# FFN of a decoder layer: one matmul per token with the high and low weight products side by side, copied out by ScalarE, summed and weighted on GpSimd

## What is computed

```python
sx, ix = top_k(sim[0], 8); sy, iy = top_k(sim[1], 8)          # 8 heads, 32 keys on each side
scores, pk = top_k(sx[..., :, None] + sy[..., None, :], 8)    # 8 of 64 pairs per head
indices = take(ix * 32 + iy, pk)                              # experts, 0 to 1023
h = gelu(einsum('bnd,bnhkd->bnhk', x, down_embed[indices]))
h = softmax(scores) * h
out = einsum('bnhk,bnhkd->bnd', h, up_embed[indices])
x = layernorm(x + out)
```

## Time and profile before

| | us |
|---|---|
| median of 3 runs (lowest, highest) | 1327.79 (1326.99, 1329.32) |
| the profiled execution: its own time | 1325.4 |
| its span | 1323.7 |
| busy in the span: PE, DVE, ACT, POOL | 1155.8, 1159.2, 865.3, 636.4 |
| the part `ffn` (from its first instruction on the chain) | 1026.96 to 1323.7 |

### The profile page before, as it was taken

The page is one execution under the profiler, slowest core; times in us unless marked ns, Lnnn a source line. Parts: engine busy times, 40 slices in busy tenths (PEclk is TensorE's granted clock), DMA queues, the critical chain, the costliest instruction groups (busy, mean ns, idle before and its releaser), DMA issues. The chain is left out here.

```text
span 1323.7 us, 32659 instructions
## 1 busy us (share of the span) xinstructions
PE 1155.8 (87%) x12752; PEld 901.2 (68%) x12752; DVE 1159.2 (88%) x2866; ACT 865.3 (65%) x1195; POOL 636.4 (48%) x534
## 2 busy tenths in 40 slices
PE   3576999999999999999999999999997739877778
PEld 2463677777777777777777777777776728767678
DVE  5797899989999899999989999998986688999984
ACT  0346888888888888988888888887974342212121
POOL 2344667566775757767566775757430310000000
PEclk9768999999999999999999999999999776666666
DMA  7006999999999999999999999999998300000000
GB/s 158 1 6 135 196 194 185 200 198 196 200 194 193 190 199 200 197 195 186 199 200 202 192 197 196 190 181 182 185 189 140 104 1 2 5 6 6 5 5 6
DMA packets 671123, 185.79 MB, mean 140 GB/s; under 512 B 655828, under 2 KB 668536, under 8 KB 670840
## 3 DMA queue, kind: packets, MB, share of 16 engines
q1 hardware_dynamic: 670968, 183.71, 81.5%
HBM read 19.51 MB, written 0.82 MB: 15 GB/s over the span
## 5 line engine op out<-in xcount | busy, mean ns | idle before, releaser
L1051 PE MATMUL ps<-pT,xa_hi 128*128 128x128 f16 x2288 | 381.1, 217 | 20.9 <-DMA pT<-p 20.6
L856 ACT ACTIVATE e<-ps,bias 128x1444 f32<-128x1444 f32 (+1 forms) x208 | 305.7, 1470 | 133.5 <-DVE bias L928 132.6
L1047 PE MATMUL ps<-pT,xa_hi 128*128 128x128 f16 x2288 | 382.8, 217 | 6.0 <-ACT uT L879 5.6
L1048 PE MATMUL ps<-pT,xa_lo 128*128 128x128 f16 x2288 | 382.8, 217 | 0.0
L926 DVE TENSOR_REDUCE nmax<-ps 128x1 f32<-128x1444 f32 (+1 forms) x208 | 343.9, 1653 | 21.0 <-PE ps L1031 20.3
L938 DVE TENSOR_TENSOR p<-e,p 128x1408 f16<-128x1408 f32 (+3 forms) x288 | 304.3, 1097 | 33.5 <-ACT p L864 32.2
L864 ACT ACTIVATE p<-e 128x1408 f16<-128x1408 f32 (+1 forms) x208 | 288.2, 1385 | 13.3
L811 POOL TENSOR_TENSOR p<-e,p 128x1408 f16<-128x1408 f32 (+1 forms) x128 | 196.6, 1557 | 182.6 <-ACT p L864 182.6
L1047 PEld LDWEIGHTS ps<-pT,xa_hi 128*128 128x128 f16 x2288 | 222.2, 98 | 30.2 <-issue 15.9
L1051 PEld LDWEIGHTS ps<-pT,xa_hi 128*128 128x128 f16 x2288 | 222.1, 98 | 27.1 <-DMA pT<-p 26.3
L1029 PE MATMUL ps<-xT_hi,q_hi 128*128 128x512 f16 (+1 forms) x624 | 229.2, 367 | 8.9 <-DMA xT_lo<-xa_lo 7.1
(11 more groups left out here) (235 smaller groups left out, 1928.2 us busy)
## 6 DMA issues: line engine op xcount, KB each, us to landing
raw<-in_ctx SPq DMA_DIRECT2D x16, 704.0 KB
pT<-p SPq DMA_TRANSPOSE x416, 4.2
f_wq<-in_L_ffn_w_q SPq DMA_DIRECT2D x1, 1024.0 KB, 5.0
f_wqt<-in_ffn_wq_t SPq DMA_DIRECT2D x2, 512.0 KB, 6.6
raw<-in_ctx SPq DMA_DIRECT2D x48, 18.0 KB
x_tok<-in_x SPq DMA_DIRECT2D x1, 800.0 KB
out_x<-ost SPq DMA_DIRECT2D x6, 128.0 KB, 2.1
wk_t<-in_wk_t SPq DMA_DIRECT2D x1, 512.0 KB, 5.4
```

Source lines behind the costliest of these rows:

```text
L856: act.activation(e32[t % E_BUF][rows, :], score_banks(t)[rows, 0:T], ACT.Exp, bias=bias[rows, t % N_BUF:t % N_BUF + 1]).then_inc(e_done, 1)
L1047: pe.matmul(out, hi, ph, start=n == 0, stop=False)
L1048: pe.matmul(out, lo, ph, start=False, stop=False)
L1051: pe.matmul(out, hi, pl, start=False, stop=False)
```

## The change

Per token column there is one matmul in place of two: the moving side is 32 columns, the high and low products side by side in one tile `mv`, and the two results are no longer summed in PSUM. A group is now 16 columns s (512 columns of PSUM), so a step has eight groups. ACT copies each group from PSUM to one of two SBUF tiles `g_sb` (`rows_out`). POOL adds the two halves (`g_sum`) and multiplies with gelu (`weigh`, two instructions per group). DVE has no part in it. The orders become:
- PE: `hidden(i,0)`, groups 0 to 3, `hidden(i,1)`, groups 4 to 7, then as before. Group g waits until group g-2 has been copied out (`g_out`), and no longer until it has been weighed.
- ACT: gelu 0, copies 0 to 3, gelu 1, `picks`, copies 4 to 7, `last_norm(i-2)`, exp, then as before. Copy g waits for POOL's sum of group g-2 (`sum_ready`).
- POOL: `combine(i)`, `norm_rstd(i-2)`, then eight times sum and product of step i-1. After the loop: the four groups of step 6, then `norm_rstd(5)`, `norm_rstd(6)`.

Two pairs of semaphores are merged into one each (`total_done` with `mean_done`, `simc_hi` with `simc_done`), with wait values to match. The core of the diff:

```diff
-        QP = 32
+        QP = 16
-        mv_hi, mv_lo = sb("mv_hi", [P, 2 * NC, PAD], F16), sb("mv_lo", [P, 2 * NC, PAD], F16)
+        mv = sb("mv_both", [P, 4 * NC, PAD], F16)
+        g_sb, g_sum = [sb(f"g_sb{i}", [P, 512]) for i in range(2)], sb("g_sum", [P, 2 * NC, QP])
...
+            def weigh(i, n):
+                nh, w = step_shape(i)
+                g, nb = group_number(i, n), nh * NC
+                both = g_sb[g % 2][:, 0:2 * nb * QP].rearrange("e (s x c) -> e x c s", x=2, c=nb)
+                pool.wait_ge(g_out, g + 1)
+                if g:
+                    pool.wait_ge(g_done, g)
+                pool.tensor_tensor(out=g_sum[:, 0:nb, :], in0=both[:, 0, :, :], in1=both[:, 1, :, :], op=ALU.add).then_inc(sum_ready, 1)
+                if n == 0:
+                    pool.wait_ge(gel_done, 2 * i + 2)
+                if i and n == 0:
+                    pool.wait_ge(y_ps, i)
+                pool.wait_ge(sum_ready, g + 1)
+                at = slice(n * QP, (n + 1) * QP)
+                pool.tensor_tensor(out=wgt[:, :, 0:nh * w].rearrange("e c (a s) -> e a c s", a=nh)[:, :, :, at],
+                                   in0=g_sum[:, 0:nb, :].rearrange("e (a c) s -> e a c s", c=NC),
+                                   in1=gel[i % 2][:, :, 0:nh * w].rearrange("e c (a s) -> e a c s", a=nh)[:, :, :, at],
+                                   op=ALU.mult).then_inc(g_done, 1)
...
+            def rows_out(i, n):
+                nh, w = step_shape(i)
+                g, used = group_number(i, n), 2 * nh * NC * QP
+                act.wait_ge(g_ps, g + 1)
+                if g >= 2:
+                    act.wait_ge(sum_ready, g - 1)
+                act.activation(g_sb[g % 2][:, 0:used], ps[:, 5 + g % 2, 0:used], ACT.Copy).then_inc(g_out, 1)
...
                 hidden(i, 0)
+                if i:
+                    for n in range(groups(i - 1) // 2):
+                        rows_out(i - 1, n)
+                hidden(i, 1)
+                picks(i)
+                if i:
+                    for n in range(groups(i - 1) // 2, groups(i - 1)):
+                        rows_out(i - 1, n)
                 if i >= 2:
                     last_norm(i - 2)
-                hidden(i, 1)
-                picks(i)
...
                 if g >= 2:
-                    pe.wait_ge(g_done, g - 1)
+                    pe.wait_ge(g_out, g - 1)
                 for q in range(QP):
                     s = n * QP + q
-                    dst = ps[:, 5 + g % 2, q * nb:(q + 1) * nb]
-                    pe.matmul(dst, oneh[0:j, :, s], mv_hi[0:j, 0:nb, s], start=True, stop=False)
-                    last = pe.matmul(dst, oneh[0:j, :, s], mv_lo[0:j, 0:nb, s], start=False, stop=True)
+                    last = pe.matmul(ps[:, 5 + g % 2, q * 2 * nb:(q + 1) * 2 * nb], oneh[0:j, :, s], mv[0:j, 0:2 * nb, s], start=True, stop=True)
```

More of the change, by code:

```diff
@@ L1067 @@
 PAD = P + 4
+STEP_GROUPS = P // 16
 def step_shape(i):
@@ L1140, in ffn @@
             sem(n) for n in ("f_waited", "fc_done", "ones_done", "x2T_ps", "x2T_done", "xcT_done"))
-        total_done, mean_ps, mean_done, xc_done, cov_ps, cov_done = (
-            sem(n) for n in ("total_done", "mean_ps", "mean_done", "xc_done", "cov_ps", "cov_done"))
+        mean_chain, mean_ps, xc_done, cov_ps, cov_done = (
+            sem(n) for n in ("mean_chain", "mean_ps", "xc_done", "cov_ps", "cov_done"))
         cw_ps, cw_done, sum_done, var_done, vrs_done, gain_done, kscaled_done = (
             sem(n) for n in ("cw_ps", "cw_done", "sum_done", "var_done", "vrs_done", "gain_done", "kscaled_done"))
-        simc_ps, simc_hi, simc_rest, simc_done = (sem(n) for n in ("simc_ps", "simc_hi", "simc_rest", "simc_done"))
+        simc_ps, simc_rest, simc_done = (sem(n) for n in ("simc_ps", "simc_rest", "simc_done"))
         simw_ps, simw_done, wide_act, wide_pool, narrow_done = (
@@ L1154, in ffn @@
         wide_idx, soft_done = sem("wide_idx"), sem("soft_done")
+        g_out, sum_ready = sem("fg_out"), sem("fsum_ready")
         block = ctx.enter_context(nc.Block())
@@ L1176, in group_number @@
         def group_number(i, n):
-            return 4 * i + n
+            return STEP_GROUPS * i + n
         def spread(v, nh):
@@ L1246, in _ @@
                     norm_rstd(i - 2)
+                if i:
+                    for n in range(groups(i - 1)):
+                        weigh(i - 1, n)
+            for n in range(groups(NSTEP - 1)):
+                weigh(NSTEP - 1, n)
             norm_rstd(NSTEP - 2)
@@ L1266, in _ @@
             act.wait_ge(simc_ps, 1)
-            act.activation(sim_c[0:1, :], ps[0:1, 6, :], ACT.Copy).then_inc(simc_hi, 1)
+            act.activation(sim_c[0:1, :], ps[0:1, 6, :], ACT.Copy).then_inc(simc_done, 1)
             def first_out(p):
@@ L1337, in _ @@
                 act.activation(w_hi[0:j, 0:w], ps[0:j, 4, 2 * P:2 * P + w], ACT.Copy).then_inc(selT_done, 1)
+            for n in range(groups(NSTEP - 1)):
+                rows_out(NSTEP - 1, n)
             last_norm(NSTEP - 2)
@@ L1342, in _ @@
         def _(dve):
-            dve.tensor_tensor(out=total[:, :], in0=x2sum[:, :], in1=x2[:, B - 1, :], op=ALU.add).then_inc(total_done, 1)
+            dve.tensor_tensor(out=total[:, :], in0=x2sum[:, :], in1=x2[:, B - 1, :], op=ALU.add).then_inc(mean_chain, 1)
             dve.wait_ge(mean_ps, 1)
@@ L1402, in _ @@
             scaled_keys(1)
[L1404 to L1416, removed]
             def norm_stats(i, part):
@@ L1502, in step @@
                 ins.then_inc(best_done, 1)
-                if i:
-                    weigh(i - 1, 2)
                 dve.wait_ge(best_done, 2 * i + 2)
@@ L1562, in step @@
                 dve.wait_ge(wlo_done, 2 * i + 1)
-                for wx, dst in ((w_hi, mv_hi), (w_lo, mv_lo)):
+                for wx, at in ((w_hi, 0), (w_lo, nb)):
                     if wx is w_lo:
                         dve.wait_ge(wlo_done, 2 * i + 2)
-                    ins = dve.tensor_tensor(out=dst[0:j, 0:nb, 0:w], in0=eqc[0:j, 0:nb, 0:w],
+                    ins = dve.tensor_tensor(out=mv[0:j, at:at + nb, 0:w], in0=eqc[0:j, 0:nb, 0:w],
                                             in1=wx[0:j, 0:w].rearrange("p (a s) -> p a s", a=1).to_broadcast([j, nb, w]), op=ALU.mult)
@@ L1574, in _ @@
             norm_shift(NSTEP - 2)
-            for n in range(groups(NSTEP - 1)):
-                weigh(NSTEP - 1, n)
             for part in range(3):
@@ L1613, in _ @@
             pe.wait_ge(cov_done, 1)
-            pe.wait_ge(mean_done, 1)
+            pe.wait_ge(mean_chain, 2)
             pe.wait_ge(wq_ld, 16)
@@ L1624, in _ @@
             sim_weights(0)
-            pe.wait_ge(simc_done, 1)
+            pe.wait_ge(simc_done, 2)
             pe.wait_ge(xcT_done, 1)
@@ L1695, in _ @@
                 if i:
-                    expert_rows(i - 1, 0)
-                    expert_rows(i - 1, 1)
+                    for n in range(groups(i - 1) // 2):
+                        expert_rows(i - 1, n)
                 hidden(i, 1)
                 if i:
-                    expert_rows(i - 1, 2)
-                    expert_rows(i - 1, 3)
+                    for n in range(groups(i - 1) // 2, groups(i - 1)):
+                        expert_rows(i - 1, n)
                 if i + 1 < NSTEP:
```

14 lines of the change are left out of this document (5 added, 9 removed).

## The result

The changed kernel takes 1351.36 us (median of 4 runs, 1350.01 to 1352.51), the kernel before 1328.55 beside it. The ratio is 1.017, with a 95% interval of 1.0149 to 1.019: slower by some 23 us, and 9 us above the upper end of my range.

A forecast was written before the change was run, and what follows sets the result against it. DVE and PE were nearly full, PE late by about 1.2 us a step. Step 1 -2.6, steps 2 to 5 +0.8 and the end +1.2 gave -0.6 on 1327.8: 1327.2 us, range 1321 to 1342 (8 in 10).

The forecast's parts named there:

- the price of POOL's instruction: POOL's sum and product per group of 256 float32 elements: 0.72 us each, a stride costing nothing to doubling.
- t: The moment from which a step is measured: the end of `mv_lo`, where PE can start the rows.
- the lock: POOL and DVE shutting each other out: the selection chain's first instruction with two SBUF inputs waits 0.4 us.
- My sign of being wrong: The forecast is wrong if DVE does not wait for `esc`, or POOL's products run beyond t + 20.
- POOL is dearer: Rival, chance 0.22: dearer sums before copy 7 delay exp and hit the selection chain; 1342 us at 0.9.
- a rival of its own (0.10): Selection chain on DVE: `idxf`, shifts and casts wait for POOL too, 0.4 us more a step; 1329 to 1331.
- PE's 8 us: Row matmuls: half of 256 a step go, freeing 8 us, but PE is late by only about 1.2.
- the end: Step 5's rows against short step 6: `oneh` 21.9 after t, last rows 7.9 us; loss 1.2 with rounding.
- Step 1: First step, without norm: exp ends at t + 15.8, `oneh` starts at about 23.4 instead of 26.0; gain 2.6.
- DVE reaches `ssum` at t + 17.5 now and could at t + 15.3: DVE loses four weighings, 2.4 us a step, three before `ssum`, but there it waits 2.7 to 3.1 for exp.

The follow-up runs named there:

- exp_first: The changed kernel, strides kept, with exp moved ahead of copies 4 to 7 in ACT's queue; 1345.96 us, 1.0122 of the kernel before.
- hi_product: Changed kernel with turned copies, four `g_sb`, groups 0 and 1 earlier on POOL, no low products, no POOL sum; 1312.16 us, 0.9878 of the kernel before.
- sum_runs: The changed kernel with POOL's sum going through the copy in its own order, leaving one strided product input; 1338.61 us, 1.0068 of the kernel before.
- early_four_flat: The changed kernel, plain copies, with four `g_sb` buffers and POOL doing group 0 before `comb`, group 1 before `frs`; 1334.03 us, 1.004 of the kernel before.
- copy_turns: The changed kernel with ACT's copy turning each group, so that POOL has no stride; 1333.49 us, 1.003 of the kernel before.

## Why the prediction was wrong

**The step that failed is the price of POOL's instruction**: "I take 0.72, as `x2sum` is the only one with two full float32 inputs and output", with the stride put at "nothing to doubling" in the bounds and at nothing in the sum. It measured 1.10 for the sum. Without strides the same sum measured 0.75, 0.73 in an undisturbed row, so the rest of the term was right: all of this term's miss is the stride. The Trainium skill (GPSIMD Engine Reference, section 3.1), which I had weighed against the rows, gives by my estimate 0.76 for this size; the unstrided 0.73 to 0.75 is close, and that estimate has nothing for a stride.

**How it grew.** Up to sum 5, at the end of which copy 7 can start, POOL ran for 11.4 us instead of 8.6 (t + 7.1 to t + 18.5). Of these 2.8 us more, six sums at some 0.38 too much make 2.3. The rest is in gaps: I took 1.5 us for a group of two instructions of 0.72; the rows show 2.1 for 1.16 and 0.73, gaps of 0.2. POOL waits for its own last result between them, and the wait for `g_done` ahead of each sum I did not price at all. Exp therefore came 3.1 us later than forecast (t + 21.5), as it stands behind copy 7 in ACT's queue, and the chain from `ssum` to the end of `sel` took 6.3 instead of 5.4, 0.5 more than the 0.4 that I had put down for the lock. Forecast t + 25.5 for `oneh`, found t + 29.1 (1206.24), against 25.3 before: four such steps are 15 us. My sign of being wrong was there: POOL's last product ran on to t + 24.1, far beyond t + 20.

**The rival was right, its weight was not.** "POOL is dearer" named the place (the sums before copy 7), the mechanism (exp behind the copies, then the lock) and the price: 1342 at an average of 0.9, some 30 us at 1.1. The average is (1.10 + 0.83) / 2 = 0.96, which would be 19 us on the line between these two; 23 were measured, and I put the rest down to the gaps. I gave it 0.22 because "the pair sums have patterns as complex and show no surcharge"; but those repeat values and write in order, and say nothing of a stride. And I cut the range at 0.9 although my own bound went to doubling.

**The lock was wider than taken.** I let it hold for the first instruction of the chain. The rows show it for a shift, a cast, a float32 subtraction (`dsc`, 1.15 in place of 0.29 in this step) and the fp16 comparisons. That was a rival of its own (0.10), and both came true together; exp_first shows how dear it is once the wait for exp no longer shields the chain.

**PE.** The matmul with 32 columns cost what I took, and most of PE's 8 us went. Their worth in the steps was about right (1.6 found, 1.2 said). At the end it was left out of the sum: PE was the bound there (before, the chain of waits runs over its row matmuls from 1280.73 until DVE's weighing at 1295.10), and 9 us were to be had, more than in steps 2 to 5 together. The changed kernel got none of them and lost 6: up to the short `oneh` its chain runs over POOL's sums and exp, as in the steps before, and after that it took 23.1 us against 23.2. I had forecast `oneh` 21.9 us after t there; it came 25.9 after (1301.8 to 1327.68), and the last rows with their four groups took 9.0 (1333.29 to 1342.28) instead of 7.9.

**Step 1** was to gain 2.6 and lost 0.8, by the same price: exp ended at t + 18.8 where I had 15.8. With the stride gone and four buffers it gained 2.2.

**DVE.** "DVE reaches `ssum` at t + 17.5 now and could at t + 15.3": it could not use it, as forecast, and hi_product shows that this holds even with a short POOL part.

What stays open: the lock and the wait for exp cannot be parted into exact sums, since each shields from the other. That they are a lock, and not two instructions that slow each other, is read from where they end, and no run tests it. Nor did I run a kernel in which DVE keeps the weighings of the last step alone, which would show whether the 9 us of the end can be had with the merged matmul.

## What to carry to other kernels

Before work goes to GpSimd, look at the access pattern that each instruction gets there, and let the engine that copies anyway (here ScalarE, out of PSUM) put the data in order. Ask what the long queue of a slow engine stands in front of: an in-order neighbour passes the delay on through its buffers, and moving the waiting instruction ahead only trades the wait for contention, unless the slow engine's work ends earlier too. And price the last, short step by its own waits; what bounds it may be another engine than in the steps before.

## What the runs showed of the hardware that I had not expected

- GpSimd's float32 addition or product of 128x256 took 0.72 to 0.75 us without strides, and the addition 1.03 to 1.07 with both inputs at a stride of 128 bytes. With one input at 64 bytes the product took 0.84 (the median in sum_runs). For 128x128 the addition took 0.45 to 0.46, and 0.68 to 0.70 with both inputs at 64 bytes.
- The strided addition had a second level. In the changed kernel's trace the 18 additions that ran for most of their time beside PE's row matmuls (L1685) took 1.10 to 1.21 us; of the 30 others 28 took 1.03 to 1.07 (the other two 1.10, and 1.83 against DVE's `eq`), and early_four_flat and exp_first show the same. What DVE did made no such difference: beside its index search it was 1.05 (1184.12), and 1.14 at 1314.08, when DVE idled and PE did not. Without strides the two levels were 0.73 to 0.75 and 0.72 to 0.73 (copy_turns). This goes together in the traces; no run tests that PE is the cause.
- ACT's copy of 128x512 from PSUM took 603 ns at a stride of 128 bytes in its input and 600 without.
- GpSimd's instructions and DVE's shifts, casts and fp16 or float32 operations on SBUF held each other up in both directions: `pij` 0.88 for 0.22, `pijf` up to 1.14 for 0.29, POOL's product 1.58 for 0.73, and once 4.78 beside `oneh` (exp_first, 1320.24).
- A fp16 matmul with 32 columns cost PE 0.065 us at a granted clock of 0.50 and 0.0625 at 1.00; 16 columns had taken 0.0625 at 0.50, and 8 had taken 0.066, in a stretch whose clock fell from 1.00 to 0.50.
